# A message-passing layer on one core: bigger rings, single buffers, paced clears and a new order of stages

## The reference

```python
h = x @ W_in2f                                   # 50000 x 256
Wij = ssp(edge_attr @ Wf1 + bf1) @ Wf2 + bf2     # edge_attr is 50000 x 64, ssp(v) = softplus(v) - log 2
Wij = Wij * edge_weight1                         # one factor per edge
x_ij = h[dst] * Wij                              # gather by dst
m = segment_sum(x_ij, src, 50000)                # scatter-add by src
m = ssp(m @ Wo1 + bo1) @ Wo2 + bo2
y = layernorm(x + (x + m))                       # over the 256 features, eps 1e-5
```

## Time and profile before

| what | value |
|---|---|
| median of 3 runs | 1865.61 us |
| the profiled execution | 1858.28 us |
| its span, first to last instruction | 1856.5 us |
| mean granted TensorE clock | 0.972 of full |
| busy share PE / DVE / ACT / POOL | 91% / 80% / 80% / 78% |
| DMA | 363.47 MB, mean 196 GB/s |

### The profile page before, as it was taken

One profiled execution on the slowest core, in us unless ns is written; L12 is line 12 of the kernel. 1 busy time (PEld: TensorE's weight loads), 2 busy tenths in 40 slices (PEclk: granted clock), 3 DMA queues, 4 the chain that ended last, 5 costly groups with the idle time before them and its releaser, 6 DMA issues. The chain is left out here.

```text
span 1856.5 us, 36676 instructions
## 1 busy us (share of the span) xinstructions
PE 1697.3 (91%) x11376; PEld 1532.2 (83%) x11376; DVE 1489.3 (80%) x3750; ACT 1492.9 (80%) x2945; POOL 1441.4 (78%) x1385
## 2 busy tenths in 40 slices
PE   3499899999999999999999998889976999999995
PEld 2378788888888888888888887778866999999995
DVE  2477788787888888888888786777765999999996
ACT  2477788778888788888888786776756999999996
POOL 7422488888887888878888888888754999999997
PEclk9699999999999999999999998999998999999998
DMA  9799866656566665666665666665675999999994
GB/s 354 251 356 372 266 123 112 126 112 125 115 125 122 112 123 114 124 125 112 125 120 116 119 122 113 114 118 108 116 185 170 333 363 362 360 360 364 357 366 174
DMA packets 177341, 363.47 MB, mean 196 GB/s; under 512 B 25622, under 2 KB 76264, under 8 KB 177148
## 3 DMA queue, kind: packets, MB, share of 16 engines
q1 hardware_dynamic: 101128, 257.75, 39.8%
q0 software_dynamic: 75136, 102.45, 32.4%
...
...
## 5 line engine op out<-in xcount | busy, mean ns | idle before, releaser
L354 POOL DMA_INDIRECT acc<-sums,src_ix x392 | 637.2, 1626 | 141.6 <-issue 116.0
L341 POOL DMA_INDIRECT xg<-in_x,dst_t x392 | 401.4, 1024 | 215.6 <-issue 114.6
L780 DVE SCALAR_TENSOR_TENSOR m_l<-pair,wgt_t,m_h 128x256 fp32r<-128x256 f32 x392 | 171.6, 479 | 230.5 <-ACT m_h L621 206.6
L385 POOL TENSOR_SCALAR sums<-sums,neg_mean,rstd 128x256 f32<-128x256 f32 x392 | 283.2, 733 | 10.2
L495 PE MATMUL pair<-m_h,same 128*128 128x256 f32 (+1 forms) x980 | 244.8, 285 | 30.4 <-ACT sums L628 21.9
L621 ACT ACTIVATE m_h<-pair,wgt_t 128x256 fp32r<-128x256 f32 x392 | 165.0, 475 | 99.5 <-PE pair L409 57.6
L495 PE MATMUL pair<-m_l,same 128*128 128x256 f32 (+1 forms) x980 | 241.8, 281 | 0.0
L409 PE MATMUL pair<-wo_h,msg_h 128*128 128x256 f32 (+1 forms) x784 | 230.9, 295 | 6.0 <-DVE m_l L780 5.2
L495 PEld LDWEIGHTS pair<-m_h,same 128*128 128x128 f32 (+1 forms) x980 | 185.1, 189 | 52.2 <-issue 34.9
L576 ACT ACTIVATE zs<-pair,bf 128x512 f32<-128x512 f32 x196 | 124.1, 685 | 125.8 <-PE pair L433 99.5
L409 PE MATMUL pair<-wo_h,msg_l 128*128 128x256 f32 (+1 forms) x784 | 222.0, 283 | 0.0
...
## 6 DMA issues: line engine op xcount, KB each, us to landing
...
attr<-in_edge_attr SPq DMA_DIRECT2D x196, 128.0 KB
...
xg<-in_x,dst_t POOLq DMA_INDIRECT x392
acc<-sums,src_ix POOLq DMA_INDIRECT x392
```

Source lines behind the costliest of these rows:

```text
L341: pool.indirect_dma_start(xg[0:g.p, g.xs, r], None, t["x"], bass.IndirectOffsetOnAxis(ap=dst_t[0:g.p, r, g.n:g.n + 1], axis=0)).then_inc(x ...
L354: pool.indirect_dma_start(acc, bass.IndirectOffsetOnAxis(ap=src_ix[g.slot][0:g.p, r:r + 1], axis=0), sums[0:g.p, g.slot, r], None, compute ...
L385: last = pool.tensor_scalar(normed[0:g.p, g.n % NRING, r], res[0:g.p, u, r], neg_mean[0:g.p, u, r:r + 1], rstd[0:g.p, u, r:r + 1], ALU.add ...
L780: dve.scalar_tensor_tensor(out=m_l[0:g.p, r], in0=bank[6][0:g.p, k * D:(k + 1) * D], scalar=col(wgt_t, r, g), in1=m_h[0:g.p, r].bitcast(F3 ...
```

## The change

It does the following:

- RING goes from 12 to 14, XRING from 11 to 17, AHEAD from 23 to 30.
- `x_h`, `x_l`, `ssp_h`, `ssp_l` and `same` exist once. The tiles `ssp`, `msg` and several small ones go; DVE writes softplus and message back into the PSUM banks that they came from, and the high and low parts are split from there. Banks 2 and 3 are held until the low part is made, and so is bank 5.
- Each clear waits until the clear four before it has landed, with one semaphore for each residue. There are 198 clears by one rule (195 and 3 before); the early eight and the wait for the first gather go.
- The loads of x for the node phase are issued inside the edge phase's last steps, 17 blocks ahead.
- All three lists of stages are new; `compare` becomes four stages.

```diff
-RING = 12
-XRING = 11
+RING = 14
+XRING = 17
-AHEAD = 23
-EARLY_CLEARS = 8
+AHEAD = 30
 FIRST_CLEARS = 36
+IN_FLIGHT = 4
 CLEARS_A_STEP = 16
...
-        x_h, x_l = (sb(n, [P, 2, H, R, P], F32R) for n in ("x_h", "x_l"))
+        x_h, x_l = (sb(n, [P, H, R, P], F32R) for n in ("x_h", "x_l"))
...
-        zs, ssp = (sb(n, [P, H, 512]) for n in ("zs", "ssp"))
-        ssp_h, ssp_l = (sb(n, [P, 2, H, R, P], F32R) for n in ("ssp_h", "ssp_l"))
+        zs, h_sb = (sb(n, [P, H, 512]) for n in ("zs", "h_sb"))
+        ssp_h, ssp_l = (sb(n, [P, H, R, P], F32R) for n in ("ssp_h", "ssp_l"))
...
-        same = sb("same", [P, 2, R * (R + 1) // 2, P], F32R)
+        same = sb("same", [P, R * (R + 1) // 2, P], F32R)
...
                 for c in range(clears, min(count, CLEARS)):
-                    sp.dma_start(acc[c * CLEAR * P:(c + 1) * CLEAR * P, :]...).then_inc(cleared, 16)
+                    a, b = c * CLEAR * P, min((c + 1) * CLEAR * P, N + R * P)
+                    wait(sp, cleared[c % IN_FLIGHT], c // IN_FLIGHT * 16)
+                    sp.dma_start(acc[a:b, :]...).then_inc(cleared[c % IN_FLIGHT], 16)
...
-            clear_to(EARLY_CLEARS)
-            sp.wait_ge(xg_in[0], 16 * R)
             clear_to(FIRST_CLEARS)
...
                 clear_to(FIRST_CLEARS + (n - 1) * CLEARS_A_STEP)
+                if G - XRING <= n - 2:
+                    fetch_x(group((n - 2) % XRING))
...
# TensorE
-                wait(pe, ssp_sb, g.n * H)                    # filter1
+                wait(pe, sspl_sb, g.n * H)
-                    wait(pe, msg_sb, g.n * H + m)            # w_of
+                    wait(pe, msgl_sb, g.n * H + m)
-            run((w_of(1), 2), (summed(0), 3), (h_of(0), 1), (summed(1), 3), (filter1, 0), (turn_x(0), 0),
-                (out1(0), 2), (turn_x(1), 0), (w_of(0), 1), (h_of(1), 1), (out1(1), 2), before={1: filter_bias})
+            run((w_of(1), 2), (summed(1), 3), (turn_x(0), 0), (turn_x(1), 0), (out1(0), 2), (h_of(0), 1), (filter1, 0),
+                (w_of(0), 1), (out1(1), 2), (h_of(1), 1), (summed(0), 2), before={1: filter_bias})
...
# ACT
-                    wait(act, h_ps, (g.n - 1) * H)           # x_high
+                    wait(act, h_ps, g.n * H)
-                    wait(act, w_ps, (g.n - 1) * H)           # ssp_high
-                    high(ssp_h[:, g.par, h], ssp[:, h].rearrange("m (r e) -> m r e", r=R), ssph_sb)
+                    wait(act, w_ps, g.n * H)
+                    high(ssp_h[:, h], bank[2 + h][:].rearrange("m (r e) -> m r e", r=R), ssph_sb)
-            run((keep_y(0), 4), (msg_high(1), 3), (ssp_high(0), 2), (ssp_high(1), 2), (keep_h(0), 2), (absolute(0), 1),
-                (absolute(1), 1), (expo(0), 1), (m_high(0), 3), (keep_y(1), 4), (expo(1), 1), (x_high(0), 1), (loga(0), 1),
-                (loga(1), 1), (x_high(1), 1), (keep_h(1), 2), (m_high(1), 3), (a_high, 0), (msg_high(0), 2), before={1: weights})
+            run((x_high(0), 1), (keep_y(0), 3), (x_high(1), 1), (ssp_high(0), 1), (msg_high(1), 2), (ssp_high(1), 1), (keep_y(1), 3),
+                (a_high, 0), (m_high(0), 2), (keep_h(0), 1), (absolute(0), 0), (absolute(1), 0), (expo(0), 0), (expo(1), 0),
+                (loga(0), 0), (loga(1), 0), (msg_high(0), 1), (m_high(1), 2), (keep_h(1), 1), before={1: weights})
...
# DVE
-                    dve.scalar_tensor_tensor(out=msg[:, m], in0=bank[5][:], scalar=bias_w[:, m:m + 1], in1=h_sb[:, m],
+                    dve.scalar_tensor_tensor(out=bank[5][:], in0=bank[5][:], scalar=bias_w[:, m:m + 1], in1=h_sb[:, m],
-                    low(msg_l[:, m], msg[:, m].rearrange("f (r e) -> f r e", r=R), msg_h[:, m], msgl_sb)
+                    low(msg_l[:, m], bank[5][:].rearrange("f (r e) -> f r e", r=R), msg_h[:, m], msgl_sb)
-                    dve.scalar_tensor_tensor(out=ssp[:, h], in0=bank[2 + h][:], scalar=neg_bf1[:, h:h + 1], in1=zs[:, h],
+                    dve.scalar_tensor_tensor(out=bank[2 + h][:], in0=bank[2 + h][:], scalar=neg_bf1[:, h:h + 1], in1=zs[:, h],
-            run((m_low(0), 3), (message(0), 2), (x_low(0), 1), (softplus(0), 1), (softplus(1), 1), (x_low(1), 1),
-                (m_low(1), 3), (message(1), 2), (a_low, 0), (msg_low(0), 2), (target, 3), (msg_low(1), 2), (ssp_low(0), 1),
-                (ssp_low(1), 1), (compare, 2), before={1: first_weights, 2: tables, 3: second_weights})
+            run((x_low(0), 1), (message(1), 2), (x_low(1), 1), (msg_low(1), 2), (ssp_low(0), 1), (ssp_low(1), 1), (a_low, 0),
+                (compare(0), 2), (m_low(0), 2), (compare(1), 2), (compare(2), 2), (message(0), 1), (compare(3), 2), (softplus(0), 0),
+                (msg_low(0), 1), (softplus(1), 0), (m_low(1), 2), (target, 2),
+                before={0: biases, 1: first_weights, 2: tables, 3: second_weights})
```

More of the change, by code:

```diff
@@ L130, in build @@
         wf1_hl = sb("wf1_hl", [P, D], F32R)
-        bf1, bf2 = (sb(n, [P, H]) for n in ("bf1", "bf2"))
+        bf1 = sb("bf1", [P, H])
+        setup = sums[:, RING - 2, 2]
+        bf2, spare_f, spare_i = setup[:, 0:H], setup[:, 8:8 + R], setup[:, 16:17].bitcast(I32)
+        bf1_two = setup[:, 24:24 + 2 * H].rearrange("p (h k) -> p h k", h=H)
         neg_bf1 = sb("neg_bf1", [P, H])
-        bf1_two = sb("bf1_two", [P, H, 2])
         bias_w = sb("bias_w", [P, H])
@@ L304, in store @@
                 sp.dma_start(rows_of(out, g).rearrange("(p r) d -> p (r d)", r=R), normed[0:g.p, u].rearrange("p r d -> p (r d)")).then_inc(stored[u], 16)
-            for n in range(G - XRING, G):
+            for n in range(G - 1, G):
                 fetch_x(group(n % XRING))
@@ L494, in stage @@
                             for m in (m_h, m_l):
-                                last = pe.matmul(o, same[0:g.p, g.par, FROM[a] + b - a, 0:g.p], m[0:g.p, a],
+                                last = pe.matmul(o, same[0:g.p, FROM[a] + b - a, 0:g.p], m[0:g.p, a],
                                                  start=a == 0 and m is m_h, stop=a == b and m is m_l)
@@ L526, in stage @@
                             for sp2, w in ((ssp2_h, wo2_h), (ssp2_h, wo2_l), (ssp2_l, wo2_h)):
-                                last = pe.matmul(o, sp2[:, g.par, h, r, 0:g.p], w[:, h, :], start=False, stop=h == H - 1 and sp2 is ssp2_l)
+                                last = pe.matmul(o, sp2[g.par][:, h, r, 0:g.p], w[:, h, :], start=False, stop=h == H - 1 and sp2 is ssp2_l)
                     last.then_inc(o_ps, 1)
@@ L609, in stage @@
                     wait(act, m_ps, g.n * 2)
-                    high(msg_h[:, m], msg[:, m].rearrange("f (r e) -> f r e", r=R), msgh_sb)
+                    high(msg_h[:, m], bank[5][:].rearrange("f (r e) -> f r e", r=R), msgh_sb)
                 return stage
@@ L682, in _, with biases @@
             low(wf1_hl[A:P], wf1[A:P], wf1_h[A:P], wf1_made)
[L684 removed]
+            def biases():
                 dve.wait_ge(b_in, 16 * 2)
```

90 lines of the change are left out of this document (44 added, 46 removed).

## The result

The changed kernel takes 1903.97 us, the median of 4 runs (1899.69 to 1907.32), against 1865.21 us in 4 runs of the kernel before: 1.021 times, 95% interval 1.0183 to 1.0237. The forecast was 1879, its own range 1860 to 1892, and 1838 to 1912 with its rivals: the direction held, the size did not, +39 us for +14. The profiled execution (span 1902.0, against 1856.5) shows where.

The account below looks back on a forecast made before the run. PE bounds the middle of the edge phase, POOL its end. F(12) 210 plus 85 steps of 13.7 plus drain 40 gave 1414.5 against 1400.35, +14 us: 1879 for the median, range 1860 to 1892, with rivals 1838 to 1912.

Parts of the forecast that it names:

- part 2: Paced clears at the start: 0.74 to 0.85 us a clear; if pacing cures the hole, clears gain up to 14 us.
- F(12): Start of group 12's filter matmuls (F(g): group g's), about 218.5 us before; forecast 210, bounds 195 to 250.
- part 1: Bigger rings: POOL has 28 gathers fewer after its first scatter, 38 us, a gain only if PE keeps up.
- Rival (c): Start not cured, hole lasts as long as gathers run or four clears are too few: F(12) near 230, 1899 us; chance 0.15.
- two of its own rivals' prices, 1820 and 1914: 1820: shorter loop, PE step 12.9 us, chance 0.28 with its 1845 case; 1914: interruptions no longer hidden, step 14.1, chance 0.12.
- POOL idle before scatters for ACT's sums through most of the phase: Sign in the edge phase that PE's longer step, not POOL, sets the pace; no size given.
- Part 3: Single buffers and PSUM in place: DVE operations take equal time, bounds -0.06 to +0.06 us per operation.
- Part 4: New order in the edge phase closes a loop of waits through PE, ACT and DVE: step 13.4 us, between 12.9 and 14.0.
- The interruptions on top: Added to each undisturbed edge step: 0.3 us, giving 13.7; they may cost 0.7 or 0.
- Rival (a): Loop shorter than counted: step 12.9 us gives 1820, step 13.3 gives 1845; chance 0.28.
- Part 5: Drain from group 97's filter matmuls to the read-back of sums: 47.0 us less 7, so 40.
- Node phase: Phase after the edge phase, ACT fully busy: same instructions, so 456 us carried over.

Follow-up runs that it names:

- e3: Changed kernel without the wait of each clear for the clear four before it: 1890.43 us, 1.0135 times the kernel before.
- e8: Changed kernel, rings and 30 ahead kept, first burst of gathers cut to 11 groups, then two per turned group: 1892.17 us, 1.0141 times the kernel before.
- e1: Changed kernel, but until group 30 two groups are gathered per turned group after a short first burst: 1861.35, 1875.1 and 1881.0 us in three batches.
- e5: Changed kernel with both edits, gathers two groups per turned group and clears unpaced: 1877.89 us, 1.0076 times the kernel before.
- e7: e1 with the stage target moved behind msg_low(1), one group later: 1866.71 us (0.9997 of the kernel before), in a later batch 1853.95 (0.9957).
- f1: Kernel before with e1's one line, gathers two groups per turned group until group 23: 1866.42 us, 0.9982 times the kernel before.

## Why the forecast was wrong

**The step that failed is part 2**: "I take 210" for F(12), with bounds 195 to 250 and a first scatter at 217. Measured 268.8 and 271.1. The forecast read the right rows: the earlier trace rows show the hole and the text says "it stands where unpaced clears and POOL's gathers both run". It then took the clears' missing pace for the cause and gave the pacing the credit of the cure, and it took 210, near the lower of its own 217 and 208. After and e3 show the opposite: the pacing does nothing for the hole (F(2) 116.6 with, 117.1 without) and costs 13 us beside it. What matters is the burst, which part 1 made longer from 12 groups to 19 by the larger ring: after, e8 and e1 in one batch, e3 and e5 in another. Rival (c) had that mechanism, "the hole lasts as long as they do", and 0.15 of the chances; but it priced it with F(12) at 230, and the upper bound of 250 was made of the clears' pace alone, with no row for a hole 40 us longer. Of the terms: 59 us too low here, 27 too high in the steps (below), 2 too high in the drain. The phase ended 30 us later than forecast. The range "with the rivals" also left out two of its own rivals' prices, 1820 and 1914.

**Part 1** said 28 gathers off POOL's path are no gain unless TensorE keeps up. Right: the last scatter waits for targets and sums from about 1190 us on. "POOL idle before scatters for ACT's sums through most of the phase" was wrong: at its first scatter ten groups of sums lay ready, and it took until then to catch up.

**Part 2's price of pacing** was 0.74 to 0.85 us a clear, 1.2 at the most. The rows of SP above give 42.23/36 = 1.17 and 22.42/16 = 1.40 beside the burst, at and over the end of the range. Not all of that is the pacing: e3's unpaced ones take 0.82 and 1.32 there. After it nine sets of 16 take 12.45 to 15.09 us, 0.87 a clear, a little over the 0.85, where e3's unpaced ones take 0.76. The fit that the forecast cites from the Trainium skill (DMA: Bandwidth & Descriptors, "Anatomy of one DMA") is stated there for DMAs that GpSimd issues; the clears are issued by SP, and with four of them in flight no set comes under 0.78 a clear, where that fit gave 0.65.

**Part 3, equal time**: held. A message written to PSUM takes 754 ns for 745 into SBUF, msg_low out of PSUM 691 for 687. These rows are of after and then of before, between 400 and 1000 us:

```profile
L767 DVE SCALAR_TENSOR_TENSOR pair<-pair,bias_w,h_sb 128x512 f32<-128x512 f32 x90 | 67.8, 754 | 40.5 <-PE pair L411 36.1 <-remote 3.2 <-issue 1.1
...
L674 DVE TENSOR_TENSOR msg_l<-pair,msg_h 128x512 fp32r<-128x512 f32 x89 | 61.5, 691 | 18.6 <-ACT msg_h L557 11.9 <-issue 3.4
```
```profile
L763 DVE SCALAR_TENSOR_TENSOR msg<-pair,bias_w,h_sb 128x512 f32<-128x512 f32 x93 | 69.3, 745 | 7.2 <-issue 4.9
...
L673 DVE TENSOR_TENSOR msg_l<-msg,msg_h 128x512 fp32r<-128x512 f32 x92 | 63.2, 687 | 2.4 <-ACT msg_h L555 2.4
```

**Part 4, the closed loop**: right. 13.4 forecast, 13.2 measured in every undisturbed step, for 12.6 before; taking one term out (e7) takes 0.3 off. The interruptions on top cost 0.2 a step, not 0.3, so the mean is 13.39 for 13.7: 27 us of luck that hid half of part 2's error. Rival (a), a shorter loop, is out.

**Part 5**: drain 37.7 for 40. **Node phase**: 457.6 for 456. Both right.

## What to carry to other kernels

A deeper ring doesn't only store more, it lets its producer run longer without a pause; ask what runs beside that burst, and try throttling it by the consumer's progress. Hold an experiment only against a run of its own batch, and ask of each what its longest wait is for: two starts of 54 us and 69 us can wait for different things. A hole in the profile that nothing explains is to be priced as growing with what the change makes longer, before it is priced as cured. And a new static order is worth following around once: the closed loop was forecast within 0.2 us from the rows of the old order, while of three attempts to shorten it two put the stage that they moved into another loop.

## What the runs showed of the chip

- While POOL issued indirect gathers without a pause (one per 1.25 us) at the start, ACT, DVE and POOL went on 10 to 60 us after the matmuls that they waited for, in four of six sets of traces, even once the 256 KB copies were done and the DMA engines were busy 0.35 of the time. Hand-overs from ACT and DVE took 0.03 to 0.2 us in the same stretch. In the other two sets (batches 1 and 5) no such delay shows under the same bursts and copies.
- So a start must be compared within a batch: the same kernel (e1) had F(12) at 227.8, 241.7 and 238.2 in three batches and took 1861, 1875 and 1881 us, and e7 took 1867 and 1854 us on one chip at two times, while the kernel before stayed at 1864 to 1868.
- An indirect scatter of 128 rows took, with the idle time before it and between 400 and 1000 us, 1.95 us in before, 1.99 in after and 2.09 in f1.
